# Two dispatch tables of a LoRA kernel: auxiliary products one slot earlier, activation loads one slot later

## The reference

```python
# x (8, 512, 2048) float32; adapter_ids, language_ids (8,)
def reference(x, adapter_ids, language_ids, A0, B0, W, Wr, A, B):
    x = x + einsum('bnr,bor->bno', einsum('bni,bri->bnr', x, B0[adapter_ids]), A0[adapter_ids])
    base   = einsum('btd,od->bto', x, W)                    # 2048 x 2048
    logits = einsum('btd,ed->bte', x, Wr) + 5 * one_hot(language_ids)
    gates  = scatter of softmax(top_2(logits))              # 8 experts
    h      = einsum('btd,erd->bter', x, A)                  # rank 16
    return x_plus = x + base + 2 * einsum('bter,bte,eor->bto', h, gates, B)
```

## Time and profile before

| | |
|---|---|
| median of 3 executions | 1626.18 us (1623.4 to 1626.25) |
| the profiled execution | 1623.4 us, span 1621.6 us |
| TensorE busy | 1587.1 us, 98% |
| VectorE busy | 1176.2 us, 73% |
| ScalarE busy | 758.7 us, 47% |
| DMA, share of 16 engines | about 79% |
| granted clock of TensorE, mean | 0.995 |

### The profile page before, as it was taken

The page is one execution under the profiler, slowest core; times in us unless marked ns, Lnnn a source line. Parts: engine busy times, 40 slices in busy tenths (PEclk is TensorE's granted clock), DMA queues, the critical chain, the costliest instruction groups (busy, mean ns, idle before and its releaser), DMA issues.

```text
span 1621.6 us, 21156 instructions
## 1 busy us (share of the span) xinstructions
PE 1587.1 (98%) x7744; PEld 1336.5 (82%) x7744; DVE 1176.2 (73%) x1599; ACT 758.7 (47%) x1000; POOL 9.8 (1%) x19
## 2 busy tenths in 40 slices
PE   7799999999999999999999999999999999999998
PEld 5687888788888888888888888888888888888887
DVE  3575444687778976888768876888769877787665
ACT  4553344344544554455444554445544544445443
POOL 1000000000000000000000000000000000000000
PEclk9899999999999999999999999999999999999999
DMA  8689797879886887879977797878877788576665
GB/s 240 190 214 252 211 241 188 214 220 239 204 220 220 220 218 197 233 224 230 219 200 230 217 232 191 234 223 224 214 200 233 222 227 205 195 234 207 207 217 161
DMA packets 396985, 351.30 MB, mean 217 GB/s; under 512 B 250522, under 2 KB 323530, under 8 KB 395850
## 3 DMA queue, kind: packets, MB, share of 16 engines
q1 hardware_dynamic: 394706, 345.76, 77.5%
q10 hardware_dynamic: 2176, 4.19, 0.9%
HBM read 280.62 MB, written 68.82 MB: 215 GB/s over the span
## 4 chain that ended last, share of the span: by engine, by line
PE 93%; DMA 2%; ACT 1%; SPq 1%; DVE 1%; issue 1%; ACTq 0%; DVEq 0%
PE pb L746 27%; PE pb L747 27%; PE pb L748 27%; PE pb L366 4%; PE pb L368 3%; PE pb L514 2%; PE pb L649 1%; SPq L625 1%; PE pb L314 1%; DMA raw<-in_L_cond_W_dram 1%; DMA wrn<-in_L_cond_Wr_dram 1%; ACT xah L342 0%; DMA t_scr<-raw 0%; DMA t_scr<-tst 0%; DMA bt_scr<-bt 0%
## 5 line engine op out<-in xcount | busy, mean ns | idle before, releaser
L742 DVE TENSOR_TENSOR wl<-raw,wh 128x1024 fp32r<-128x1024 f32 (+1 forms) x456 | 555.1, 1217 | 333.9 <-ACT wh L738 333.7
L738 ACT CAST wh<-raw 128x1024 fp32r<-128x1024 f32 (+1 forms) x456 | 477.1, 1046 | 683.7 <-PE pb L748 675.6
L746 PE MATMUL pb<-wh,sh 128*128 128x512 f32 x1568 | 612.8, 391 | 0.5 <-DVE ost L782 0.5
L747 PE MATMUL pb<-wl,sh 128*128 128x512 f32 x1568 | 611.6, 390 | 0.0
L748 PE MATMUL pb<-wh,sl 128*128 128x512 f32 x1568 | 611.2, 390 | 0.0
L748 PEld LDWEIGHTS pb<-wh,sl 128*128 128x128 f32 x1568 | 294.3, 188 | 62.8
L746 PEld LDWEIGHTS pb<-wh,sh 128*128 128x128 f32 x1568 | 294.6, 188 | 56.2 <-DVE wl L742 0.9
L747 PEld LDWEIGHTS pb<-wl,sh 128*128 128x128 f32 x1568 | 294.6, 188 | 55.0
L366 PE MATMUL pb<-awb,xah 128*128 128x304 f32 x512 | 138.4, 304 | 2.9 <-DVE aux L381 1.6
L368 PE MATMUL pb<-awb,xal 128*128 128x256 f32 x512 | 134.4, 280 | 0.0
L746 PE MATMUL pb<-wh,xh 128*128 128x512 f32 x256 | 106.2, 415 | 1.2 <-DVE ost L782 0.8
(11 more groups left out here) (135 smaller groups left out, 1280.6 us busy)
## 6 DMA issues: line engine op xcount, KB each, us to landing
raw<-t_scr SPq DMA_DIRECT2D x392, 512.0 KB, 4.4
xst<-in_x_dram SPq DMA_DIRECT2D x768, 32.0 KB, 3.7
raw<-in_L_cond_W_dram SPq DMA_DIRECT2D x128, 128.0 KB, 3.9
t_scr<-tst SPq DMA_DIRECT2D x32, 512.0 KB, 5.1
raw<-bt_scr SPq DMA_DIRECT2D x28, 512.0 KB, 3.9
out_dram<-ost SPq DMA_DIRECT2D x28, 512.0 KB, 4.4
out_dram<-u SPq DMA_DIRECT2D x28, 512.0 KB, 3.4
t_scr<-raw SPq DMA_DIRECT2D x32, 256.0 KB, 4.1
```

Of the source, the lines that this page charges most:

```text
L738: e.copy(pair_split(wh, g), pair_source(g)).then_inc(c_wh, 1)
L742: e.tensor_tensor(out=pair_split(wl, g), in0=pair_source(g), in1=pair_split(wh, g).bitcast(f32), op=ALU.subtract).then_inc(c_wl, 1)
L746: e.matmul(o, h, wh[:, g % RING, k, :], start=start, stop=False)
L747: e.matmul(o, h, wl[:, g % RING, k, :], start=False, stop=False)
```

## The change

Two tables that say in which slot something is issued are shifted by one slot: the aux products of unit u stand at `X_AT + 2` in place of `X_AT + 3` (slots 6, 7, 10, 11, ... 34, 35 in place of 7, 8, 11, 12, ... 35, 36), and the parts of the x blocks 2 to 7 are issued at slots 6 to 29 in place of 5 to 28. Nothing else is touched; `aux_low` and `aux_sum` stay in iteration 21 (and 37).

```diff
         X_AT = {4 * (u // 2) + 4 + u % 2: u for u in range(16)}
-        AUX_AT = {at + 3: u for at, u in X_AT.items()}
-
-        LOAD_AT = {4 * m - 3 + a: (m, a) for m in range(2, 8) for a in range(4)}
+        AUX_AT = {at + 2: u for at, u in X_AT.items()}
+
+        LOAD_AT = {4 * m - 2 + a: (m, a) for m in range(2, 8) for a in range(4)}
```

## The result

The changed kernel takes 1645.4 us in the median of 4 executions (1644.35 to 1647.75), against 1626.2 before: ratio 1.0125, 95% interval 1.0107 to 1.0142. It is slower by 19.2 us. The forecast was 1640.0 (1633 to 1651). The profiled execution took 1641.07 us with a span of 1639.3, that is 17.7 more than the profiled one before.

A forecast was written before the change was run, and what follows sets the result against it. TensorE's instruction stream was taken to bound images 1 to 7, so any new wait adds in full: six stalls of 2.30 us, 13.8 us, all other terms 0, on 1626.2 give 1640.0 us; range 1633 to 1651.

The forecast's parts named there:

- The place and the count: At slot 22 of images 1 to 6, unit 8 restarts banks 4 and 5 and waits for the unmoved aux_sum: six stalls.
- The size: Each stall at slot 22: 2.30 us, including 0.06 of signal and 0.10 of restart; six make 13.8 us.
- The deadline alone: Rival at slot 22: VectorE's chain does not shift, 1.57 us per stall, 9.4 us in all, 1635.6 us; chance 0.10.
- the shift of VectorE's chain: Slot 19 ends 1.05 us later; VectorE's idle time swallows 0.32, so aux_sum ends 0.73 us later.
- The x loads: Parts issued one slot later: VectorE waits 3 us at unit 12's transpose, hidden before slot 30 by 1.2 us; price 0.
- blocks 2 to 5 have more slack: Later x loads of blocks 2 to 5 and 7 have no adapter rows before them, so more slack than block 6.
- x_lo of unit 0 at slot 6: VectorE's x_lo ends at 540.90, slot 6 starts at 541.18: fits by 0.28 us, price 0; 1.8 us if missed by 0.3.
- the clock: Granted clock behind each new gap of about 2.0 us at slot 22: no fall in the sum; a fall costs 1.7 us.
- the rival with falls behind all six gaps: Half clock for a stretch after every slot 22 gap: 10.3 us more, 1650.3 us; chance of falls after most gaps 0.13.
- main case: Six stalls at slot 22, clock lost after no or few gaps: 1640.0 us; chance 0.62.
- nearer to the one without a fall: The 2.0 us gap lies between idle 1.83 us (clock stayed 1.00) and 2.78 us (0.57), nearer the former.
- No matmul ran ahead: Rival at slot 22: its twelve products run ahead of the wait, nothing lost, 1626.2 us; chance 0.07.

The follow-up runs named there:

- e9: The changed kernel unaltered, timed once more on one chip beside the one with the aux products alone: 1642.8 us, ratio 1.0102 to the kernel before the change.

## Why the prediction was right, and what was off

**The place and the count.** Forecast: unit 8 waits for aux_sum at slot 22 of images 1 to 6, because aux_sum did not move. Shown: six waits on line 381; gone with unit 8 back in slot 23, and gone with aux_sum moved one iteration up.

**The size.** Forecast 2.30 us each, idle time 2.0; measured 2.39 and 2.06. Both parts of it hold. The deadline alone was put at 1.57: with units 0 to 7 left where they were and the old loads, the time rose by 1635.25 - 1625.56 = 9.7 us, 1.6 for each image. The rest, forecast at 0.73, is the shift of VectorE's chain by the moved long slot: the gap grows from 1.31 to 2.06, by 0.75.

**The x loads.** Forecast: VectorE waits 3 us at the transpose of unit 12 and no one waits for it. In image 2 of the changed kernel this wait is in the timeline:

```profile
621.55 0.71 DVE L262 STREAM_TRANSPOSE pool_a<-xst 128x512 f32<-128x512 f32 x1 [2.94 <-DMA xst<-in_x_dram]
...
623.29 0.68 DVE L347 TENSOR_TENSOR xal<-pool_a,xah 128x512 fp32r<-128x512 f32 x1
...
625.31 0.30 PE L366 MATMUL pb<-awb,xah 128*128 128x304 f32 x1
```

x_lo of unit 12 ends at 623.97, and slot 30 starts at 625.31 without waiting: 1.3 us to spare, against 1.2 forecast. The loads alone cost nothing. Wrong is the prediction's sentence that blocks 2 to 5 have more slack: block 4 feeds unit 8, in the very chain that ends in aux_sum. In image 5 this transpose waited 2.35 us, and the gap grew to 2.43:

```profile
1158.64 0.71 DVE L262 STREAM_TRANSPOSE pool_a<-xst 128x512 f32<-128x512 f32 x1 [2.35 <-DMA xst<-in_x_dram]
```

The price is 0.4 us in one image; between the two kernels timed side by side it cannot be seen.

**x_lo of unit 0 at slot 6.** The margin was put at 0.28 us and measured at 0.27 (544.88 less 543.92 + 0.69). It held.

```profile
543.92 0.69 DVE L347 TENSOR_TENSOR xal<-pool_b,xah 128x512 fp32r<-128x512 f32 x1
...
544.88 0.30 PE L366 MATMUL pb<-awb,xah 128*128 128x304 f32 x1
```

**The term that was mis-sized: the clock.** The sum had 0 for it, and the rival with falls behind all six gaps had 10.3 us. The truth lies between: behind a gap of 2.06 to 2.09 us the clock fell in 8 of 23 cases, at 1.5 to 1.6 us each where the forecast said 1.7. This is two falls and 3.2 us in the profiled execution. The forecast's main case allowed for "a few" such gaps, but its 1640.0 holds none, and so it came out low. The reading "nearer to the one without a fall" took the idle time of 1.83 us that was not followed by a fall for more than it was, one single case; an idle time of 1.89 us in another run was followed by one. By these runs the sum needed a mean of two falls, 3.2 us, and would have been 1643.

**What is left.** The median of the result is 19.2 us above the kernel before. The six stalls are 14.3 of it, two falls 3.2 and the longer gap 0.4, if its executions had what the profiled one had; the other 1.3 us are not explained, and no profile shows a third fall. Timed once more (e9), the same kernel was 17.2 us above the one before, and six stalls and two falls make 17.5. Executions also differ ahead of the first gap: in the two profiled ones of the changed kernel, each with two falls, the first restart stands at 409.44 and at 411.50:

```profile
411.50 0.41 PE L366 MATMUL pb<-awb,xah 128*128 128x304 f32 x1 [2.07 <-DVE aux L381]
```

The first stage, which the change does not touch, can thus make 2 us of difference between two executions. The prediction's 1640.0 is 5.4 us below the median of 1645.4. The upper end of its range, 1651, came from the case with six falls; two were seen. The place, the count and the size of the stall were forecast; the clock's share lay inside the range without being forecast, which is in part luck.

**No matmul ran ahead.** Slot 22's dense products stood behind the wait and ran after it: between 596.72 and 599.17 TensorE starts nothing.

## What to carry to other kernels

When the engine that sets the time never waits, an earlier slot for its work has nothing to win and can cost. Before moving a consumer up, list every producer it waits for and where that one stands in its own engine's order; the one that restarts an accumulation also waits for the reader of the last one, and both must move together. And moving long slots shifts the start of whatever is queued behind them on the other engines; here that cost half as much again as the late deadline itself (a gap of 2.06 us in place of 1.31). A gap put in front of TensorE costs its length and a little more (2.39 us for an idle time of 2.06), and at 2 us and more it sometimes costs a stretch at half clock as well.

## What the runs showed of the hardware that was not expected

The same gap of 2.06 us, at the same place of the program, was followed by a fall of the clock in one image and not in the next. Among the gaps in front of unit 8 the share rises with the length: 0 of 12 up to 1.68 us, 8 of 24 from 2.06 to 2.43, 4 of 6 at 2.67, 6 of 6 from 3.20 us. A fall costs 1.5 to 1.6 us of time here. The length is not all: image 1 had a fall behind each of its four gaps of 2.06 or 2.07 us, and in the first stage one run had a fall behind 1.89 us and another none behind 2.70 us. What else decides is open.

The Trainium skill (TensorE: Matmul & The Clock Gate, section Why this matters for your kernels) warns of idle gaps of more than about 3 us between bursts of matmuls. The runs agree for the six gaps of 3.20 to 3.32 us, and differ below: 12 of the 30 gaps of 2.06 to 2.67 us were followed by a fall. So the warning that the forecast names speaks, by its words on the page, of longer gaps than this one, and here the runs decide.
